# GpSimd rotates the queries and keys of the odd batches of the first attention beside VectorE

## The reference

```python
q = (einsum('bsd,ed->bse', x, Wq) + bq)  # 16 heads of 16
k = (einsum('bsd,ed->bse', x, Wk) + bk)  # 4 heads of 16
v = (einsum('bsd,ed->bse', x, Wv) + bv)  # 4 heads of 16
q = _rms_norm(q); k = _rms_norm(k)       # t * rsqrt(mean(t*t) + EPS)
q = _apply_rope(q, cos, sin)             # [t1*cos + t2*sin, -t1*sin + t2*cos]
k = _apply_rope(k, cos, sin)
q = q * q_gain
attn = softmax(causal(einsum('bhqd,bhkd->bhqk', q * scale, k)))
out = einsum('bhqk,bhkd->bqhd', attn, v) @ Wo.T + bo
x = _layernorm(x + out)
```

## Time and profile before

| | us |
|---|---|
| median of 3 runs | 509.61 |
| lowest and highest of them | 508.43, 509.75 |
| the profiled execution, its own time | 509.1 |
| its span, first instruction to last | 507.4 |
| PE busy | 404.9 (80%) |
| DVE busy | 349.4 (69%) |
| ACT busy | 239.8 (47%) |
| POOL busy | 99.1 (20%) |

### The profile page before, as it was taken

How to read it: one execution, slowest core, us unless ns; L and a number is a source line. 1 busy time by engine, 2 the same in 40 slices (tenths; PEclk the granted TensorE clock), 3 DMA queues, 4 the chain that set the end, 5 groups by cost and what they waited for, 6 DMA issues and landing times.

```text
span 507.4 us, 8072 instructions
## 1 busy us (share of the span) xinstructions
PE 404.9 (80%) x3090; PEld 315.9 (62%) x3090; DVE 349.4 (69%) x802; ACT 239.8 (47%) x420; POOL 99.1 (20%) x103
## 2 busy tenths in 40 slices
PE   1906478998884664599998688999986899999993
PEld 1506445676653552388766565666765788888883
DVE  0489698777877968476648879656946485666545
ACT  1558714665433653466567713546536324422220
POOL 4400005439401030051183000000002700000000
PEclk9967598999997757579999989999999899999998
DMA  6900020000000000000000005970000000000101
GB/s 203 295 6 1 1 70 5 3 3 2 2 2 0 1 1 0 0 1 1 1 1 1 1 1 79 122 150 3 1 2 1 0 1 1 0 1 1 43 1 41
DMA packets 13125, 13.32 MB, mean 26 GB/s; under 512 B 2904, under 2 KB 12448, under 8 KB 12832
## 3 DMA queue, kind: packets, MB, share of 16 engines
q1 hardware_dynamic: 12224, 12.54, 11.0%
q10 hardware_dynamic: 864, 0.27, 0.2%
HBM read 11.56 MB, written 1.05 MB: 25 GB/s over the span
## 4 chain that ended last, share of the span: by engine, by line
PE 62%; DVE 21%; ACT 11%; issue 3%; DMA 1%; POOL 1%; SPq 0%; DVEq 0%; POOLq 0%; ACTq 0%
PE PS L2135 12%; PE PS L2152 6%; ACT arena L743 6%; PE PS L1750 4%; PE PS L1834 4%; DVE mx L1250 3%; PE PS L1728 3%; PE PS L2062 3%; PE PS L2075 3%; PE PS L1875 3%; PE PS L381 3%; PE PS L1802 2%; PE PS L1844 2%; PE PS L1631 2%; PE PS L1782 2%
## 5 line engine op out<-in xcount | busy, mean ns | idle before, releaser
L862 ACT ACTIVATE PT<-PS 128x512 f32<-128x512 f32 x96 | 53.5, 594 | 36.0 <-PE PS L1802 35.9
L2135 PE MATMUL PS<-arena_r 128*128 128x512 f32 x264 | 66.0, 399 | 2.2 <-ACT xT L743 2.2
L664 POOL TENSOR_SCALAR va<-mv 128x4 f32<-128x4 f32 x12 | 5.3, 441 | 274.9 <-DVE mv L1086 274.9
L743 ACT ACTIVATE arena<-PS 96x1024 bf16<-96x1024 bf16 (+4 forms) x59 | 44.4, 807 | 27.7 <-PE PS L1728 12.9
L2135 PEld LDWEIGHTS PS<-arena_r 128*128 128x128 f32 x264 | 49.2, 193 | 12.2 <-issue 2.6
L1728 PE MATMUL PS<-ident,arena 128*96 128x128 bf16 x416 | 32.3, 249 | 28.8 <-DVE arena L1129 27.5
L1728 PEld LDWEIGHTS PS<-ident,arena 128*96 128x96 bf16 x416 | 30.5, 148 | 32.5 <-DVE arena L1129 29.1
L1750 PE MATMUL PS<-masks,ident 128*128 128x512 bf16 x112 | 43.0, 384 | 4.7 <-DVE mx L1250 2.4
L1250 DVE TENSOR_REDUCE mx<-PS 128x4 f32<-128x1024 f32 x32 | 39.0, 1220 | 1.2 <-PE PS L1782 0.2
L2152 PEld LDWEIGHTS PS<-arena_r 128*128 128x128 f32 x264 | 34.4, 191 | 2.5 <-DVE arena_r L1553 0.9
L2152 PE MATMUL PS<-arena_r 128*128 128x256 f32 x264 | 35.1, 283 | 0.7 <-DVE arena_r L1553 0.7
(11 more groups left out here) (218 smaller groups left out, 904.1 us busy)
## 6 DMA issues: line engine op xcount, KB each, us to landing
arena<-in_L_ffn_w SPq DMA_DIRECT2D x16, 176.0 KB, 9.6
arena<-in_L_ffn_w SPq DMA_DIRECT2D x2, 1024.0 KB, 11.1
arena<-in_L_ffn_w SPq DMA_DIRECT2D x2, 704.0 KB, 6.2
arena<-in_fside_BxS2xS SPq DMA_DIRECT2D x1, 1024.0 KB, 12.3
out<-x SPq DMA_DIRECT2D x4, 256.0 KB, 2.6
x<-in_x SPq DMA_DIRECT2D x1, 768.0 KB, 8.7
arena<-in_L_attn_Wq SPq DMA_DIRECT2D x2, 256.0 KB, 4.4
arena<-in_L_attn_Wo SPq DMA_DIRECT2D x2, 256.0 KB, 6.5
```

Of the source, the lines that this page charges most:

```text
L743: return nc.scalar.activation(dst, src, ACT.Copy)
L862: nc.scalar.activation(PT[:, n % 2, 512 * j:512 * (j + 1)], bank(3 + j), ACT.Exp, scale=NEG_SCALE)\
L2135: last = mm(bank(2 * (n % 2) + gu), wp[c][:, gu, c_ * P:(c_ + 1) * P], xp[5][:, c, blk * 512:(blk + 1) * 512], start=(step == 0 and c == 0 ...
```

## The change

Two things are changed. First, the seven instructions of `rotate` for batches 1 and 3 are issued by GpSimd, in the same form, instead of VectorE; VectorE signals `qk_normed` when a pair has been normed, GpSimd signals `odd_batches_rotated`, and `hi_part` of an odd batch waits for that. Second, the orders on ScalarE and VectorE are changed around it: `hi, mid, hi, mid` instead of `hi, hi, mid, mid` on ScalarE, and on VectorE `read_projections(2)` in front of the first `rem_part`, `thresholds()` between the two `rem_part` of the second pair, `lo_part(0, b)` in front of `read_projections(3)`, which must now wait until GpSimd has read `qk[:, 1]`.

```diff
+            def rotate(b):
+                pool.wait_ge(qk_normed, b // 2 + 1)
+                pool.wait_ge(w["const"], LOADS["const"])
+                if b >= 2:
+                    pool.wait_ge(A[0]["lo"], b - 1)
+                hf = HD // 2
+                for k in range(2):
...
+                    pool.tensor_tensor(ri, qi, cos, ALU.mult)
+                    pool.tensor_tensor(si[:, :, 0:hf], qi[:, :, hf:HD], s1, ALU.mult)
+                    ins = pool.tensor_tensor(si[:, :, hf:HD], qi[:, :, 0:hf], s2, ALU.mult)
+                alone(ins)
+                ro, sq = (z[:, b % 2].rearrange("p t n -> p (t n)") for z in (qro, qsq))
+                alone(pool.tensor_tensor(ro, ro, sq, ALU.add), odd_rotated)
+            rotate(1)
+            rotate(3)
...
                     for b in (0, 2):
                         hi_part(L, b)
+                        mid_part(L, b)
                         hi_part(L, b + 1)
-                        mid_part(L, b)
                         mid_part(L, b + 1)
...
-                act.wait_ge(a["sq"], u + 1) if L == 0 else act.wait_ge(a["proj"], u + 1)
+                if L == 1:
+                    act.wait_ge(a["proj"], u + 1)
+                elif u % 2 == 0:
+                    act.wait_ge(a["sq"], u // 2 + 1)
+                else:
+                    act.wait_ge(odd_rotated, u // 2 + 1)
...
                         normed_queries_and_keys(b)
                         rotate(b)
-                        rotate(b + 1)
-                        rem_part(0, b)
-                        rem_part(0, b + 1)
                         if b == 0:
                             read_projections(2)
+                        rem_part(0, b)
+                        if b == 2:
+                            thresholds()
+                        rem_part(0, b + 1)
+                        lo_part(0, b)
+                        if b == 0:
+                            dve.wait_ge(odd_rotated, 1)
                             read_projections(3)
-                        else:
-                            thresholds()
-                        lo_part(0, b)
                         lo_part(0, b + 1)
```

More of the change, by code:

```diff
@@ L271, in post_ln_decoder_two_layers @@
         kept = sem("kept_by_causality")
+        qk_normed = sem("qk_normed")
+        odd_rotated = sem("odd_batches_rotated")
         out_read = sem("out_read")
@@ L671, in smooth_roots @@
                 alone(pool.tensor_scalar(qs[:, 1, 0:n], qs[:, 2, 0:n], Q_EPS, None, ALU.max), root_ready)
+            def rotate(b):
[5 more added lines that the diff above has]
+                for k in range(2):
+                    qi, ri, si = (z[:, b % 2, k, :].rearrange("p (h d) -> p h d", d=HD) for z in (qk, qro, qsq))
+                    cos = rope[:, k, 0, :].unsqueeze(1).to_broadcast([P, HEADS0, HD])
+                    s1 = rope[:, k, 1, 0:hf].unsqueeze(1).to_broadcast([P, HEADS0, hf])
+                    s2 = rope[:, k, 1, hf:HD].unsqueeze(1).to_broadcast([P, HEADS0, hf])
+                    pool.tensor_tensor(ri, qi, cos, ALU.mult)
[6 more added lines that the diff above has]
+            rotate(3)
             def below(k, lo, hi):
@@ L1182, in normed_queries_and_keys @@
                 q3 = q2.rearrange("p (h d) -> p h d", d=HD)
-                link(v.tensor_tensor(q3, q3, qrs[:, :].unsqueeze(2).to_broadcast([P, 4 * HEADS0, HD]), ALU.mult))
+                v.tensor_tensor(q3, q3, qrs[:, :].unsqueeze(2).to_broadcast([P, 4 * HEADS0, HD]), ALU.mult).then_inc(qk_normed, 1)
+                dve.wait_ge(qk_normed, b0 // 2 + 1)
             def rotate(b):
```

## The result

The changed kernel took 517.17 us in the median of its first four executions (515.75 to 523.96) against 509.68 for the kernel before beside them; the quotient of the medians is 1.0147. Predicted were 517.2 us and +1.5%. The kernel before varies by itself with the granted TensorE clock of the whole execution: in 25 executions beside the first experiments it had spans of 512.1 to 513.7 us at a mean clock of 0.898 and of 506.4 to 509.4 at 0.917 and more, with five in between.

What follows compares the result with a forecast made beforehand. A VectorE-ScalarE chain in the first attention's front was taken as the bound. Turns and new order sum to 2X + 1.6 = +7.6 us, 516.7 on the profiled execution, 517.2 us (+1.5%) with 0.5 for the median; range 512.0 to 521.5.

Steps and rivals of the forecast that it cites:

- Where the front stands in the chain: First attention's front, 20 to 57 us: on the chain, with a fixed sequence behind, so its shift moves the end.
- GpSimd's prices: GpSimd's rotation of odd batches: products at 0.5 and 0.87 us plus waits for a turn, sum 1.5 us more.
- the 5.6: Upper bound in us of the delay of VectorE's rotation, at the dearer GpSimd price.
- Turns (X): VectorE and GpSimd alternate on two-input SBUF instructions, delaying VectorE's rotation of each pair by X = 3.0 us.
- The order: ScalarE's hi, mid, hi, mid makes it wait for VectorE twice; hi(2) to second burst 8.5 us instead of 7.0.
- The sum: Second TensorE burst starts at 64.7 instead of 57.14, +7.6 us, on profiled span 507.4 and own time 509.1.
- 2X + 1.6: Shift of second burst: (X + 0.9) first pair, (X - 0.8) second pair's rotation, 1.5 from hi(2) to burst.
- X = 0: Lower bound: VectorE and GpSimd don't wait for each other; the new order alone still costs 2.1 us.
- Hardly wait for each other: Rival on the rotations: X from 0 to 2.4, +2.1 to +6.4 us, 511.7 to 516; chance 0.16.
- dearer GpSimd: Rival: GpSimd costs more or gets more turns, X 4 to 5.6, +9.6 to +12.8 us; chance 0.14.
- hidden: Rival: the front isn't on the path that sets the end, time as before, 509.6 us; chance 0.03.
- The clock rival: Second burst and stretch from 75.60 at full TensorE clock: 3.8 us less, 507.9 at X = 0; chance 0.03.

Runs made afterwards that it cites:

- e7b: Kernel before with 36 tiny chained idle instructions on VectorE in front of the second pair's thresholds(); burst +7.5 us, ratio 1.0154.
- e3: Changed kernel with the cosine and sine tables that VectorE's rotation products read moved to PSUM; burst +3.6 us, ratio 1.0107.
- e8b: Changed kernel run again unchanged, on the same chip as the plain delay; burst +6.7 us, ratio 1.0163 to the kernel before.
- e4: Changed kernel, but GpSimd starts its rotation only when VectorE's of the same pair has ended; burst +4.4 us, ratio 1.0030.
- e6b: e3 with ScalarE's old order and lo_part behind read_projections(3), thresholds() still between the remainders; burst -0.4 us, ratio 1.0016.
- e1: Changed kernel with GpSimd still rotating odd batches, but ScalarE's and VectorE's orders of the kernel before; burst +3.5 us, ratio 1.0034.
- e5b: Kernel before, GpSimd idle, with thresholds() between the second pair's remainders and woT's copy behind its middle parts; burst -0.8 us, ratio 0.9999.

## Why the prediction was right, point by point

- **Where the front stands in the chain.** Right. e7b shows that 7.5 us in front of the burst are 7 to 8 us of time.
- **GpSimd's prices.** Right: 0.86, 0.51 and 1.54 us without a turn to wait for (e3) for predicted 0.87, 0.52, 1.56. The upper end for short runs of numbers isn't needed; runs of 8 and 16 cost nothing extra here. (That upper end was also summed wrongly: the 5.6 has the dearer price on the products and not on the sum of 640, which would be 0.45 more, so about 6.0.)
- **Turns (X).** The mechanism was right, the size too large: 2.48 us (5.18 - 2.70) for 3.0. The mis-sized term is how long GpSimd holds a turn, and the fault was in reading the rows at 227 us. This is the VectorE instruction in front of the one at 227.96:

```profile
227.36 0.68 DVE L1466 TENSOR_TENSOR arena_r<-arena,arena_r 128x512 fp32r<-128x512 f32 x1
```

It ends at 228.04; VectorE's next row starts 0.08 before that. I let GpSimd's turn begin at that next start (0.67 us to 228.63), but counted VectorE's own turn from end to end (0.56), so each turn that passed from VectorE to GpSimd had 0.08 us counted twice. From end to end GpSimd's turn is 0.59, 0.14 less than its 0.73, and the profile after shows the same: 0.72 for 320 numbers (29.57 - 28.85) and 0.38 for 160 (30.13 - 29.75), 0.14 less than the 0.86 and 0.52 that they take without a turn to wait for. Over six products the 0.08 is 0.5 us, nearly the whole miss. The trace of the kernel before held the right number. VectorE was first in line and also got its sum in front of GpSimd's, as assumed. The Trainium skill (SBUF — State Buffer, "SBUF: two separate sides") says that a VectorE instruction with two SBUF inputs excludes a GpSimd one that reads SBUF, and that one with at most one SBUF input, outside the 2-port modes that VectorE's copies and casts can enter, doesn't. e3 agrees, in both halves.
- **The order.** Right in kind: the two waits of 1.10 and the burst's longer run-up. From hi(2) to the burst it is 64.14 - 55.56 = 8.6 us, predicted 8.5.
- **The sum.** 2X + 1.6 gives 6.6 us with the measured X; the burst moved by 6.7. I had said 7.6. It also holds term by term, less the 0.3 us that were there before: the norm of the second pair 3.35 later (43.84 for 40.19) for X + 0.9 = 3.4, ScalarE's high part of batch 2 5.1 later (55.56 for 50.17) for 5.1, and 1.6 for the 1.5 behind it. That the median hit 517.2 so closely is partly luck: with a shift of 6.7 the working gives a span of 514.1, and the executions at a clock of 0.912 to 0.915 show that (514.0 and 515.3; in e8b 513.4 and 514.3); the executions of lower clock lift the median.
- **X = 0 is not to be had by moving GpSimd's work alone.** I gave +2.1 for it. e3 and e4, the nearest to it, have +3.6 and +4.4, because VectorE's remainders then fall in GpSimd's turns. At the X of the change they don't, so the forecast didn't need this; its lower bound did.
- **The rivals.** "Hardly wait for each other" is out by the profile after, "dearer GpSimd" by e3, "hidden" by e7b. The clock rival was no way to a gain from here, but its effect exists: the 80 transposes took 7.06 us in the changed kernel at a granted clock of 0.64 in that stretch, 6.77 at 0.67 in e8b, which is the same kernel, and 6.03 at 0.76 in e6b (0.5 is 1.2 GHz, 1 is 2.4 GHz). I had held against this rival that TensorE idles longer in front of the burst. The profiles don't bear that out: after 9.43 us of idle time the burst took 7.09 us at 0.64 in the kernel before and, after 9.42, 6.03 in e6b; after 16.93 us in e7b it took 6.44 at 0.71.

What was given away by parts: the turns and the order cost about as much each. Taking the order back (e1) saves 3.2 us of the 6.7, taking the turns off the products (e3) 3.1, and both, with thresholds() early, 7.1 (e6b). The early place of thresholds() is worth some of that: in e5b it and woT's move gave 0.8.

Left open: why VectorE's instruction at 82.41 in the kernel before came through 1.7 us ahead of the end of GpSimd's instruction beside it. It is no accident of one execution: the changed kernel has the same pair at 89.38 (1.07 us) and 89.30 (2.86). No run tried it; all turns of the rotation were instruction by instruction. The rows just in front of it show another thing that I overlooked:

```profile
81.70 0.64 POOL L687 TENSOR_SCALAR_AFFINE_SELECT PT<-PT 128x512 f32<-128x512 f32 x1
81.82 0.55 DVE L1319 CAST mst<-mxr 128x32 bf16<-128x32 f32 x1
```

This copy to bf16 reads only one tensor in SBUF, and yet it took 0.55 us where the median of its line is 0.18, and ended 0.03 behind GpSimd's instruction. So "two inputs in SBUF" is the condition that e3 shows for the products of this change, not the only one under which VectorE waits.

## What to carry to other kernels

An idle engine is only a second pair of hands if it doesn't need what the first one holds: look in the trace for a place where both ran the same kinds of instruction side by side, and read when the one ended against the other, from end to end. If they take turns, the first engine's half lasts as long as its own turns and the other's together (5.18 us here, where both halves on VectorE take 5.3). Reading one of the operands from PSUM took the products out of the turns in e3. And before interleaving two items on an engine (`hi, mid, hi, mid`), ask what its queue waits for at each place: a ready item behind a waiting one costs the whole wait.

## What the runs showed of the hardware

- VectorE products with both inputs in SBUF alternated with GpSimd's, one instruction each (changed kernel, e1, e8b); with one input in PSUM neither lost more than 0.02 us (e3).
- From end to end GpSimd's turn was 0.14 us shorter than its instruction alone (0.72 of 0.86, 0.38 of 0.52), VectorE's as much (0.18 of 0.32).
- A VectorE copy to bf16 with one SBUF input waited for GpSimd too: 0.55 us for 0.18 (kernel before, 81.82; changed kernel, 88.79).
- The mean granted clock of a whole execution of the kernel before went from 0.898 to 0.928 in the 25 executions, and the span from 513.7 to 506.4 us (7.3). That is as much as the change itself, so that intervals over 10 executions of e1 and e4 still hold 1.000 where their profiles and their executions of like clock show +3 us.
